# A graph network on one core: the order of three steps per window on two engines of the last stage

## The chip, the cores and the metric

One core of a Trainium2 chip runs the whole program as one launch. The metric is the device time of one execution in microseconds (us); the kernel before the change takes 5778.91 us (median of 3 runs, 5777.4 to 5779.42). The engines are TensorE (PE for matmuls, PEld for weight loads), VectorE (DVE), ScalarE (ACT), GpSimd (POOL) and SyncE (SP). DMAs are issued from the queues of ACT, POOL and SP.

## The reference

Four graph layers follow each other, each as `x = x + layer(relu(layernorm(x)))`, over 6250 nodes of 128 features and 100000 edges that are sorted by their target node `dst`. Only the last layer matters here:

```python
x_src = x[src]
msg = zeros((E, 128))
for r in range(4):                       # four kinds of edge
    hr = x_src @ weight[r] + bias[r]
    msg = where((rel == r)[:, None], hr, msg)
agg = segment_max(msg, dst, num_segments=n)     # the largest message of each target node
agg = where((deg > 0)[:, None], agg, 0)
out = x + x @ weight[4] + bias[4] + agg
```

The targets are drawn as `6250 * u ** 2`, so that low node numbers have many edges each and high ones few.

## The kernel before

A projection first writes all four products of every node into the table `y_tab` in DRAM. The last stage, which starts near 4780 us of the span, then makes the segment maximum. The edges are cut into GN = 112 groups of GE = 896 (7 tiles of 128), the nodes into NT = 49 blocks of 128. A *window* (called step `s` or `i` in the code) is one pair of a group and a block that share an edge; there are SN = 112 + 49 - 1 = 160 windows. A group whose edges all go to one block has one window, a group in which a block ends has two. As the edges thin out towards high nodes, two windows per group become more frequent towards the end.

What is done for a window `s`, and where:

- POOL gathers the 7 x 128 rows of a group from `y_tab` into a ring in `arena` that holds RG = 8 groups, with 7 indirect DMAs (L2709), and tells when the group has landed (L2703). It may overwrite a ring place once SP has seen the last window of that group staged (L2729 to L2731).
- ACT `stage_group(s)` (L2872): waits until the group has landed, then copies it from the ring to one of two buffers `staged_t`. Two windows of one group are staged twice.
- ACT `load_mask(s)` (L2879): a DMA of the row of segment borders, after the scan two windows earlier.
- PE `turn(s)` (L2835): 7 transposes to PSUM (`pa` or `pb` in turns).
- DVE `scan(s)` (L2777): a running maximum along the edges, which restarts at the borders that the mask marks. `carry_on` hands the last column on, `build(s)` (L2791) makes the 0/1 matrix that picks the last edge of each node.
- PE `back(s)` (L2842): 7 transposes of the scanned rows back to PSUM (`pc`).
- ACT `keep_back(s)` (L2883): copies them to one of two buffers `kept_t`.
- PE `select(s)` (L2849): 7 accumulating products, recorded as 14 matmuls, that move the row of each node's last edge to its node (`pd`). It waits for `keep_back(s)`, for `build(s)` and for `add(s-1)`.
- DVE `add(s)` (L2798) adds them to `x`; ACT `store(s)` (L2888) writes the block to `out`.

Each engine runs its own list in the order in which `body(i, b)` calls these functions, through `walk_steps` (L686): five calls written out, a hardware loop over pairs of windows, six calls written out. An engine does not pass over an instruction that waits. So the list sets who is held up by whom. On ACT the list of `body(i)` is stage(i+2), load_mask(i+2), keep_back(i), store(i-2). On PE it is turn(i+1), back(i), select(i-1). On DVE it is scan(i), add(i-2), carry_on(i), build(i). `window_values` (L680) at the head of ACT's body reads three numbers of the window (block, ring place, group to wait for) from a table into registers.

Of the kernel before, what the change touches and what calls it, by code (L numbers as in the profile page):

```python
# [123 lines left out]
def build(nc, a, out):  # L124
    assert QL % 2 == 0 and NT % NG == 0 and GN % RG == 0
    groups = NT // NG
    with ExitStack() as ctx:
# [221 lines left out]
        def wait_apart(engine, sem, value):  # L349


            engine.wait_ge(sem, value)
            engine.sem_inc(passed, 1)  # L353
# [311 lines left out]
        def after(engine, c, n):  # L665

            if not (isinstance(n, int) and n <= 0):
                engine.wait_ge(c.sem, c.past(n))

        def inside(s):  # L670
            return not isinstance(s, int) or 0 <= s < SN

        def loaded_values(kind, at, bounds):

            why = "the walk tables are made on the chip from counts below these bounds"
            _, values = nc.values_load_multi_w_load_instructions(at, engines=(kind,), skip_runtime_bounds_check_because=why)
            return [nc.s_assert_within(value, low, high, skip_runtime_bounds_check_because=why)
                    for value, (low, high) in zip(values, bounds)]

        def window_values(kind, table, w, first, bounds):  # L680

            last = first + len(bounds)
            at = table[0:1, w, first:last] if isinstance(w, int) else table[0:1, bass.ds(w, 1), first:last].rearrange("o w k -> o (w k)")
            return loaded_values(kind, at, bounds)

        def walk_steps(engine, body):  # L686

            for i in range(-1, 4):
                body(i, i % 2)
            with engine.Fori(2, SN // 2 - 1) as pair:  # L690
                for b in range(2):
                    body(pair * 2 + b, b)
            for i in range(SN - 2, SN + 4):
                body(i, i % 2)
# [1580 lines left out]
        with nc.Block() as block:  # L2275
# [31 lines left out]
            def _(dve):  # L2307
# [142 lines left out]
                def body(w):  # L2450
# [14 lines left out]
                    if next_here:  # L2465
                        tile, _, back = window_values(mybir.EngineType.DVE, walk_rows, w + 1, 4 * WT, AHEAD2)
                        run(w + 1, steps)
                        chain(w + 1, steps, tile, back)
# [228 lines left out]
        with nc.Block() as block:  # L2697
# [121 lines left out]
            @block.tensor  # L2819
            def _(pe):  # L2820
                def tables():
                    pe.wait_ge(table_in.sem, table_in.past(1))
                    nc.tensor.matmul(pa[:, 0:SN], ones[0:1, :], on_row, start=True, stop=True).then_inc(table_on.sem, 1)

                def relative():
                    tail = SN - P
                    pe.wait_ge(table_in.sem, table_in.past(2))
                    for j in range(GT):
                        to = (pa, pb)[j // 4][:, j % 4 * 2 * P:(j % 4 + 1) * 2 * P]
                        nc.tensor.transpose(to[:, 0:P], rel_rows[0][:, j * P:(j + 1) * P], ident[:, :])  # L2830
                        ins = nc.tensor.transpose(to[:, P:SN], rel_rows[1][0:tail, j * P:(j + 1) * P], ident[0:tail, 0:tail])
                    ins.then_inc(table_on.sem, 1)
                    pe.wait_ge(table_in.sem, table_in.past(3))

                def turn(s, b):  # L2835
                    after(pe, edge_staged, s + 1)
                    after(pe, edge_scanned, s - 1)
                    for t in range(GT):
                        ins = nc.tensor.transpose(turned_ps[b][:, t * P:(t + 1) * P], staged_t[b][:, t * P:(t + 1) * P], ident[:, :])  # L2839
                    ins.then_inc(edge_turned.sem, 1)  # L2840

                def back(s, b):  # L2842
                    after(pe, edge_scanned, s + 1)
                    after(pe, edge_kept, s)
                    for t in range(GT):
                        ins = nc.tensor.transpose(back_ps[:, t * P:(t + 1) * P], run_t[b][:, t * P:(t + 1) * P], ident[:, :])  # L2846
                    ins.then_inc(edge_back.sem, 1)

                def select(s, b):  # L2849
                    after(pe, edge_kept, s + 1)  # L2850
                    after(pe, hot_built, s + 1)
                    after(pe, block_added, s)
                    for t in range(GT):
                        ins = nc.tensor.matmul(last_ps, hot[b][:, t * P:(t + 1) * P], kept_t[b][:, t * P:(t + 1) * P],  # L2854
                                               start=(t == 0), stop=(t == GT - 1))
                    ins.then_inc(block_summed.sem, 1)

                def body(i, b):
                    if inside(i + 1):
                        turn(i + 1, 1 - b)  # L2860
                    if inside(i):
                        back(i, b)
                    if inside(i - 1):
                        select(i - 1, 1 - b)

                tables()
                relative()
                walk_steps(pe, body)

            @block.scalar  # L2870
            def _(act):
                def stage_group(s, b, start, need):  # L2872
                    after(act, edge_turned, s - 1)
                    wait_apart(act, group_landed.sem, group_landed.past(need))
                    nc.scalar.copy(staged_t[b].rearrange("p (t d) -> p t d", d=D),  # L2875
                                   ring[:, bass.ds(start, GT * RW)].rearrange("p (t w) -> p t w", w=RW)[:, :, 0:D]
                                   ).then_inc(edge_staged.sem, 1)

                def load_mask(s, b, need):  # L2879
                    after(act, edge_scanned, s - 1)  # L2880
                    act.dma_start(mask_t[b], cut_row[0:1, bass.ds((need - 1) * GE, GE)].broadcast_to([P, GE])).then_inc(mask_loaded[b].sem, 16)

                def keep_back(s, b):  # L2883
                    after(act, edge_back, s + 1)
                    after(act, block_summed, s - 1)
                    nc.scalar.copy(kept_t[b], back_ps).then_inc(edge_kept.sem, 1)  # L2886

                def store(s, j):  # L2888
                    after(act, block_added, s)
                    after(act, block_stored, s * 16)  # L2890
                    act.dma_start(out[bass.ds(j * P, P), :], x[:, bass.ds(j, 1), :].rearrange("p j d -> p (j d)")  # L2891
                                  ).then_inc(block_stored.sem, 16)

                STEP = [(0, NT - 2), (0, (RG - 1) * GT * RW), (1, GN)]

                def body(i, b):
                    if not isinstance(i, int) or 0 <= i < SN + 2:
                        j, start, need = window_values(mybir.EngineType.Activation, scalar_walk, i, 0, STEP)
                    if inside(i) and inside(i + 2):
                        stage_group(i + 2, b, start, need)  # L2900
                        load_mask(i + 2, b, need)
                    if inside(i):
                        keep_back(i, b)
                    if inside(i - 2):
                        store(i - 2, j)

                act.wait_ge(walk_laid.sem, walk_laid.past(1))
                for s in range(2):
                    start, need = loaded_values(mybir.EngineType.Activation, pe_walk[0:1, s, :], STEP[1:3])
                    load_mask(s, s, need)  # L2910
                    stage_group(s, s, start, need)
                walk_steps(act, body)
                act.wait_ge(block_stored.sem, block_stored.past(SN * 16))

# [20 lines left out]
```

## Time and profile before

| | us |
|---|---|
| median of 3 runs | 5778.91 |
| the profiled execution | 5778.91 |
| its span, first to last instruction | 5776.9 |
| last stage, first gather to the end of the span (4783.2 to 5776.9) | 993.7 |

Over the whole span PE is busy 61%, DVE 56%, ACT 34% and POOL 67%. The mean granted clock of TensorE is 0.78 of full speed, where 1.0 is the level of 2.4 GHz and 0.5 that of 1.2 GHz. In rows of a timeline, the first number is the start in us from the span's start, the second the duration; `xN` counts the instructions merged into a row, and the bracket gives the idle time of the engine before it with what ended the wait. A busy engine is not one that sets the time; the waits and the chain that ended last tell that.

### The profile page before, as it was taken

To read this page: it belongs to the slowest core of one execution; us is meant where nothing else is said; L and a number is where in the kernel's file an instruction comes from. 1 tells how busy PE (TensorE), PEld (TensorE's weight loads), DVE (VectorE), ACT (ScalarE), POOL (GpSimd) and SP (SyncE) were. 2 spreads that over 40 slices of the span, in tenths; PEclk is the share of its full clock that TensorE was granted. 3 is DMA by queue.
4 is the path that set the end of the run, shared out by engine and by line. 5 is a ranking of instruction groups with operands and counts; after the bars stand their busy time and mean duration, and the time that the engine had idled before them with its cause. 6 is when DMAs were issued, how large, how long until landed. Compare 5 with 4: busy or idle time off the path is not lost. (4 is left out here: it accounts for less than half of the span.)

```text
span 5776.9 us, 98732 instructions
## 1 busy us (share of the span) xinstructions
PE 3537.5 (61%) x18635; PEld 3062.3 (53%) x18636; DVE 3228.5 (56%) x8215; ACT 1946.2 (34%) x6380; POOL 3869.1 (67%) x4036
## 2 busy tenths in 40 slices
PE   3445556544455643889999887234555574666677
PEld 3444455544455532677777745233454544656676
DVE  4233344444455655788888863334555564455677
ACT  2111111111122211566777654123334441222333
POOL 4777777677777757777777102777777707777776
PEclk9666777766667766999999997567767787788889
DMA  4222222211111112344443220222222223333333
GB/s 124 61 61 63 64 65 65 74 52 53 52 53 52 53 38 74 107 113 116 120 118 114 88 83 23 52 53 54 53 53 52 51 79 97 93 96 101 104 112 104
DMA packets 347571, 439.10 MB, mean 76 GB/s; under 512 B 129314, under 2 KB 243822, under 8 KB 347359
## 3 DMA queue, kind: packets, MB, share of 16 engines
q0 software_dynamic: 129056, 262.08, 17.3%
q1 hardware_dynamic: 148596, 117.11, 6.4%
q10 hardware_dynamic: 69819, 58.90, 3.5%
q14 instruction: 77, 0.63, 0.0%
q8 instruction: 23, 0.38, 0.0%
HBM read 324.58 MB, written 113.18 MB: 76 GB/s over the span
## 5 line engine op out<-in xcount | busy, mean ns | idle before, releaser
L1000 PE MATMUL pa<-arena,weighted 128*128 x4480 | 866.2, 369 | 860.6 <-POOLq L719 478.4
L1000 PEld LDWEIGHTS pa<-arena,weighted 128*128 128x128 f32 x4480 | 800.1, 274 | 915.1 <-issue 915.0
L2709 POOL DMA_INDIRECT arena<-y_tab,y_idx x784 | 741.6, 946 | 395.8 <-issue 218.3
L1405 POOL DMA_INDIRECT arena<-t_tab,src_idx x784 | 778.7, 993 | 265.6 <-issue 215.8
L725 POOL DMA_INDIRECT arena<-h_tab,src_idx x784 | 743.8, 949 | 306.2 <-issue 219.5
L2288 POOL DMA_INDIRECT arena<-t_tab,src_idx x784 | 755.3, 963 | 245.0 <-issue 219.7
L725 POOL DMA_INDIRECT arena<-sage_tab,src_idx x784 | 741.0, 945 | 261.9 <-issue 214.2
L2529 PE MATMUL pa<-weighted 128*128 128x130 f32 x2240 | 421.4, 364 | 21.2 <-ACT weighted L2607 11.3
L2529 PEld LDWEIGHTS pa<-weighted 128*128 128x128 f32 x2240 | 391.7, 270 | 34.5 <-issue 19.0
L870 DVE SCALAR_TENSOR_TENSOR scan_t<-scan_t,alpha,pa 128x130 f32<-128x130 f32 x320 | 110.2, 344 | 501.7 <-PE pb L1007 351.6
L2875 ACT COPY arena<-arena 128x896 f32 x160 | 150.1, 938 | 685.7 <-POOLq L2703 613.1
L430 POOL DMA_INDIRECT start_rows<-nodeval,start_idx x98 | 101.2, 1032 | 411.7 <-DVE nodeval L2203 338.6
L862 DVE TENSOR_TENSOR weighted<-pd,rel 128x896 f32<-128x896 f32 x320 | 348.0, 1088 | 51.2 <-issue 44.6
L1045 ACT COPY out_rows<-pb 128x128 f32<-128x128 f32 x320 | 84.9, 265 | 822.3 <-PE pb L1007 701.0
L1761 PE MATMUL pa<-weighted 128*128 128x264 f32 x976 | 316.3, 407 | 58.1 <-ACT weighted L1834 38.7
L1834 ACT ACTIVATE weighted<-arena,weighted 128x128 f32 x976 | 317.4, 390 | 64.6 <-POOLq L1396 49.8
L1761 PE MATMUL pa<-arena,weighted 128*128 128x264 f32 x976 | 301.6, 391 | 50.7 <-DVE arena L1567 39.1
L2607 ACT ACTIVATE weighted<-arena,weighted 128x64 f32 x1280 | 323.0, 335 | 19.7
L2854 PE MATMUL pd<-arena,weighted 128*128 128x128 f32 x2240 | 321.9, 303 | 0.6 <-DVE x L2804 0.6
L2854 PEld LDWEIGHTS pd<-arena,weighted 128*128 128x128 f32 x2240 | 313.2, 222 | 0.8 <-issue 0.7
L1834 ACT ACTIVATE arena<-arena 128x128 f32 x976 | 307.9, 389 | 14.6
L1050 ACT ACTIVATE scan_t<-scan_t 128x128 f32<-128x128 f32 x320 | 99.0, 309 | 591.3 <-DVE scan_t L887 591.3
(553 smaller groups left out, 7440.0 us busy)
## 6 DMA issues: line engine op xcount, KB each, us to landing
gat_tab<-out_rows SPq DMA_DIRECT2D x244, 260.0 KB
mask<-cut_row ACTq DMA_DIRECT2D x160, 224.0 KB
arena<-t_tab,src_idx POOLq DMA_INDIRECT x1568
arena<-h_tab,src_idx POOLq DMA_INDIRECT x784
arena<-sage_tab,src_idx POOLq DMA_INDIRECT x784
y_tab<-arena SPq DMA_DIRECT2D x49, 256.0 KB, 2.3
arena<-y_tab,y_idx POOLq DMA_INDIRECT x784
arena<-gat_tab SPq DMA_DIRECT2D x12, 1040.0 KB, 5.0
```

The source lines that it names most:

```text
L725: nc.gpsimd.indirect_dma_start(out=rows[:, g % RG * GT + t, 0:D], out_offset=None, in_=table[:, :], in_offset=bass.IndirectOffsetOnAxis(ap ...
L862: v.tensor_tensor(hot[b].rearrange("p (t n) -> p t n", n=P), node_row.unsqueeze(1).broadcast_to([P, GT, P]), at.unsqueeze(2).broadcast_to( ...
L1000: ins = nc.tensor.matmul(pa[:, b * CE:b * CE + RW], hot[b][:, t * P:(t + 1) * P], ring[:, bass.ds(start + t * RW, RW)], start=(t == 0), st ...
L1405: nc.gpsimd.indirect_dma_start(out=rows[:, g % QR * QT + t, :], out_offset=None, in_=t1_tab[:, :], in_offset=bass.IndirectOffsetOnAxis(ap= ...
L1761: nc.tensor.matmul(pa[:, b * CE:b * CE + HALF], one, flow1[b][:, t * YW:t * YW + HALF], start=(t == 0), stop=(t == QT - 1))
L1834: ins = nc.scalar.activation(flow1[b][:, at:at + D], ring1[:, bass.ds(start + t * TW, D)], ACT.Copy, scale=flow1[b][:, t * YW + 2 * D + hd ...
L2288: nc.gpsimd.indirect_dma_start(out=rows[:, g % RB * GT + t, :], out_offset=None, in_=t2_tab[:, :], in_offset=bass.IndirectOffsetOnAxis(ap= ...
L2529: ins = nc.tensor.matmul(pa[:, b * CE:b * CE + BW], hot2[b][:, t * P:(t + 1) * P], flow[b][:, t * BW:(t + 1) * BW], start=(t == 0), stop=( ...
L2607: ins = nc.scalar.activation(flow[b][:, at:at + HD], ring2[:, bass.ds(start + t * BW + hd * HD, HD)], ACT.Copy, scale=flow[b][:, at + HD:a ...
L2709: nc.gpsimd.indirect_dma_start(out=edge_rows[:, g % RG * GT + t, 0:D], out_offset=None, in_=y_tab[:, :], in_offset=bass.IndirectOffsetOnAx ...
L2854: ins = nc.tensor.matmul(last_ps, hot[b][:, t * P:(t + 1) * P], kept_t[b][:, t * P:(t + 1) * P], start=(t == 0), stop=(t == GT - 1))
L2875: nc.scalar.copy(staged_t[b].rearrange("p (t d) -> p t d", d=D), ring[:, bass.ds(start, GT * RW)].rearrange("p (t w) -> p t w", w=RW)[:, : ...
```

## The change

Two lists are reordered, and nothing is added or removed. On PE, `select(i-1)` comes before `back(i)`. On ACT, `stage_group(i+2)` goes from the head of `body(i)` to its end, behind `load_mask(i+2)`, `keep_back(i)` and `store(i-2)`.

```diff
@@ PE
                 def body(i, b):
                     if inside(i + 1):
                         turn(i + 1, 1 - b)
+                    if inside(i - 1):
+                        select(i - 1, 1 - b)
                     if inside(i):
                         back(i, b)
-                    if inside(i - 1):
-                        select(i - 1, 1 - b)
@@ ACT
                     if inside(i) and inside(i + 2):
-                        stage_group(i + 2, b, start, need)
                         load_mask(i + 2, b, need)
                     if inside(i):
                         keep_back(i, b)
                     if inside(i - 2):
                         store(i - 2, j)
+                    if inside(i) and inside(i + 2):
+                        stage_group(i + 2, b, start, need)
```

PE in the loop over pairs of windows, before. L2839 is `turn`, L2846 `back`, L2854 `select`; L668 are the registers of their waits.

```order
L2839 MATMUL pb<-ident,arena 128x128 x7
L668 REGISTER_ALU
L2846 MATMUL pc<-ident,weighted 128x128 x7
L668 REGISTER_ALU x2
L2854 MATMUL pd<-arena,weighted 128x128 x7
L668 REGISTER_ALU
L2839 MATMUL pa<-ident,arena 128x128 x7
L2846 MATMUL pc<-ident,weighted 128x128 x7
L668 REGISTER_ALU
L2854 MATMUL pd<-arena,weighted 128x128 x7
```

The same place after the change:

```order
L2839 MATMUL pb<-ident,arena 128x128 x7
L668 REGISTER_ALU x2
L2854 MATMUL pd<-arena,weighted 128x128 x7
L668 REGISTER_ALU
L2846 MATMUL pc<-ident,weighted 128x128 x7
L668 REGISTER_ALU
L2839 MATMUL pa<-ident,arena 128x128 x7
L668 REGISTER_ALU
L2854 MATMUL pd<-arena,weighted 128x128 x7
L2846 MATMUL pc<-ident,weighted 128x128 x7
```

`back` is now the last of the three for each window, directly ahead of the next `turn`.

ACT in the last written-out call ahead of the loop, before. L676 reads the window's numbers, L2875 is `stage_group`, L2881 `load_mask`, L2886 `keep_back`, L2891 `store`.

```order
L676 TENSOR_LOAD alpha
L352 REGISTER_ALU
L2875 ISA
L2875 COPY arena<-arena 128x896
L2881 ISA
L2881 DMA mask<-cut_row 128x896
L2886 COPY arena<-pc 128x896
L2891 ISA
L2891 DMA out<-x 128x128
```

The same call after the change:

```order
L676 TENSOR_LOAD alpha
L2881 ISA
L2881 DMA mask<-cut_row 128x896
L2886 COPY arena<-pc 128x896
L2891 ISA
L2891 DMA out<-x 128x128
L352 REGISTER_ALU
L2875 ISA
L2875 COPY arena<-arena 128x896
```

The staging copy, with its waits (L352 and the ISA row), now stands behind the copy that waits for `back`.

## Rows read from the trace of the kernel before

**Rows 1.** The page: the span, and the gathers of the last stage.
```profile
span 5776.9 us, 98732 instructions
...
L2709 POOL DMA_INDIRECT arena<-y_tab,y_idx x784 | 741.6, 946 | 395.8 <-issue 218.3
```

**Rows 2.** The chain that ended last, in order of time: start, us, what.
```profile
5757.04 4.61 DMA arena<-y_tab,y_idx
```

**Rows 3.** Waits from 4820 us on: engine and line, releaser, us, times, longest.
```profile
ACT arena L2875 <- POOLq L2703: 590.7, 106, 7.1
DVE weighted L2782 <- DMA mask<-cut_row: 276.3, 90, 5.4
```

**Rows 4.** Stretches of 87.5 us, the staging copies alone (x): busy us, granted clock.
```profile
5061.80:5149.30 87.50, 12.19 (x13) 0.83 0.34 96
5149.30:5236.80 87.50, 13.14 (x14) 0.76 0.36 100
...
5324.30:5411.80 87.50, 14.08 (x15) 0.83 0.37 103
5411.80:5499.30 87.50, 15.02 (x16) 0.85 0.37 107
5499.30:5586.80 87.50, 15.96 (x17) 0.88 0.37 110
...
5674.30:5761.80 87.50, 16.89 (x18) 0.95 0.43 114
```

**Rows 5.** The same view, all: PE, PEld, DVE, ACT, POOL busy (instructions), clock.
```profile
4886.80:4974.30 87.50, 55.10 (x310) 52.90 (x309) 40.78 (x55) 19.29 (x22) 66.16 (x70) 0.75 0.31 90
4974.30:5061.80 87.50, 54.90 (x342) 52.13 (x341) 44.16 (x60) 21.04 (x24) 66.18 (x70) 0.79 0.33 93
5674.30:5761.80 87.50, 66.21 (x529) 61.69 (x527) 68.89 (x95) 31.62 (x36) 63.32 (x67) 0.95 0.43 114
```

**Rows 6.** Timeline near the end, at full clock: start, us, engine, line, operation.
```profile
5750.92 0.94 ACT L2875 COPY arena<-arena 128x896 f32 x1 [4.17 <-POOLq L2703]
...
5751.91 0.98 PE L2839 MATMUL pb<-ident,arena 128*128 128x128 f32 x7 [1.53 <-ACT arena L2875]
...
5752.81 0.95 PE L2846 MATMUL pc<-ident,weighted 128*128 128x128 f32 x7
...
5753.60 1.73 PE L2854 MATMUL pd<-arena,weighted 128*128 128x128 f32 x14
...
5755.16 0.93 PE L2839 MATMUL pa<-ident,arena 128*128 128x128 f32 x7
```

**Rows 7.** Timeline: a `back` that `keep_back` waits for, and the store behind it.
```profile
5727.29 1.70 PE L2846 MATMUL pc<-ident,weighted 128*128 128x128 f32 x7
...
5729.11 0.91 ACT L2886 COPY arena<-pc 128x896 f32<-128x896 f32 x1 [0.63 <-PE pc L2846]
5729.44 0.37 ACTq L2891 DMA_DIRECT2D out<-x  x1
```

**Rows 8.** Timeline of ACT near the stage's start: a staging copy right behind a `keep_back`.
```profile
4824.37 0.91 ACT L2886 COPY arena<-pc 128x896 f32<-128x896 f32 x1 [2.04 <-PE pc L2846]
4825.35 0.94 ACT L2875 COPY arena<-arena 128x896 f32 x1
```

**Rows 9.** Timeline of PE: `turn` after idle times of three lengths.
```profile
4841.85 0.98 PE L2839 MATMUL pa<-ident,arena 128*128 128x128 f32 x7 [1.87 <-ACT arena L2875]
...
4911.77 1.75 PE L2839 MATMUL pa<-ident,arena 128*128 128x128 f32 x7 [2.90 <-ACT arena L2875]
...
5016.83 1.10 PE L2839 MATMUL pa<-ident,arena 128*128 128x128 f32 x7 [2.56 <-ACT arena L2875]
```

**Rows 10.** Timeline of the end: the last staging, `keep_back` behind it, the last `select`.
```profile
5761.89 0.94 ACT L2875 COPY arena<-arena 128x896 f32 x1 [6.42 <-POOLq L2703]
...
5762.73 0.90 ACT L2886 COPY arena<-pc 128x896 f32<-128x896 f32 x1
...
5771.84 1.80 PE L2854 MATMUL pd<-arena,weighted 128*128 128x128 f32 x14 [0.58 <-DVE x L2804]
```

## The prediction

> **What bounds the kernel now.** Read the page first: the span, and the group of gathers of the last stage [rows 1]. 784 gathers, 946 ns each and mostly 0.3 us of issue between them, are 1.25 us apiece, so a group of 7 lands every 8.75 us. Then the chain that ended last: from about 4783 us on it is made of these gathers, down to the last one, which lands at 5757.04 + 4.61 = 5761.65 [rows 2]. So POOL sets the pace of the whole stage, and what follows the last landing is a tail of 15 us [rows 10]. The waits say the same from the other side: ACT's staging copy waits 590.7 us in 106 waits for the mark that a group has landed [rows 3]. The scans wait another 276.3 us for the mask DMA, but this lies inside the same slack.
>
> How much slack the consumers have is read from the stretches [rows 4]: in 87.5 us ten groups land, and 14 windows are staged in a stretch at 5149 to 5237, 18 in the last (13, 14, 14, 15, 16, 17, 17, 18 in the eight from 5061.8 on; one of each pair of equal counts stands in the rows). So a window may cost 87.5 / 14 = 6.25 us early and only 87.5 / 18 = 4.86 us at the end. Before 5061.8 the counts are lower still, since fewer groups have two windows. DVE needs 68.89 / 18 = 3.8 us per window [rows 5] and PE, at full clock, 0.90 + 0.79 + 1.56 = 3.25 us from `turn` to `turn` [rows 6]. Both fit.
>
> **What the change does to the loop.** Before, ACT stages window i+2 ahead of `keep_back(i)`; the staging is held up only by the landing. A `turn` is therefore ready whenever data is, and PE's three pieces of a window can run into those of the next. After, the staging of i+2 waits behind `keep_back(i)`, which waits for `back(i)`, and PE does `back(i)` last, behind `turn(i+1)` and `select(i-1)`. The next thing on PE is `turn(i+2)`, which needs that staging. This closes a ring through two engines in which nothing overlaps: turn, select, back, keep_back, staging, turn. Its period, term by term at full clock:
>
> - turn to select: 0.90 us, as from `turn` to the piece behind it, 5751.91 to 5752.81 [rows 6].
> - select to back: 1.56 us, as from `select` to the piece behind it, 5753.60 to 5755.16 [rows 6].
> - back to keep_back: the 7 transposes take 0.95 us [rows 6], and `keep_back` starts 0.12 us after their end (5727.29 + 1.70 = 5728.99, then 5729.11) [rows 7]. Together 1.07 us.
> - keep_back to staging. The trace has no staging queued behind a store. From below: 0.84 us, the distance of two copies when the second is ready (5761.89 to 5762.73) [rows 10]. From above: 0.98 us (4824.37 to 4825.35), where the table read stood between [rows 8]. The store is issued 0.33 us after `keep_back` starts and takes 0.37 us on ACT's queue [rows 7], and the waits of the staging come behind it, so I take 0.93.
> - staging to turn: 0.99 us, 5750.92 to 5751.91 [rows 6].
>
> The sum is 5.45 us per window, 5.36 to 5.50 by the bounds. The DVE's 3.8 us fit in it. The store and its wait for `add(i-2)` cost nothing: that add is needed by `select(i-1)`, which precedes `back(i)`. The mask DMA now goes out one staging earlier and is not waited for: the 276.3 us of waits should fall to nearly nothing, and win nothing, being cover under POOL. The table read of the next window is under the 3.5 us in which ACT waits for PE. On SP only the wait for `edge_staged` is touched; the ring of 8 groups gives 70 us before POOL is held up, and then POOL is late because the consumers are, not the reverse.
>
> 5.45 us is above 4.86 and below 6.25. So the windows fall behind the landings towards the end, and the backlog at the last landing is the largest value of (windows staged since some moment) x period - (time since). With 5.45 over the last 3 stretches, 52 windows: 283.4 - 262.5 = 21 us; a start inside a stretch adds up to one more window, some 25 us.
>
> **The clock in this loop.** In each period PE has one idle piece, 0.12 + 0.93 + 0.99 = 2.04 us, after 3.41 us of work. After 1.87 us of idle, `turn` still took 0.98 us, the high level (2.4 GHz); after 2.56 us it took 1.10, partly low, after 2.90 us 1.75, the low level (1.2 GHz) [rows 9]. So 2.04 lies between, nearer to the end without a fall. What speaks for a fall: the 1.87 stood alone behind work, whereas here the idle comes back each period and PE is busy 3.41 / 5.45 = 63%. The stretches in which PE is busy 55.10 / 87.5 = 63% got 0.75 and 0.79 of the clock [rows 5], though with longer idles. I take 0.79 as the granted share, 42% of the time at the low level. If that time lay all over PE's work, each us of it would lose half: period 5.45 / 0.79 = 6.90 us. Spread evenly over work and idle it is 2.04 + 3.41 / 0.79 = 6.36 us. A fall comes of an idle piece and so hits the work behind it; I take 6.8. With this the backlog is, over 7 stretches, 111 windows: 754.8 - 612.5 = 142.3 us; over 8 stretches, with 13 windows more: 843.2 - 700 = 143.2 us. Further back a stretch has under 87.5 / 6.8 = 12.9 windows and adds nothing. That is above 70 us, so POOL waits too, for the first time in this stage.
>
> The Trainium skill, TensorE: Matmul & The Clock Gate, weighs both ways. Its section "HAM oscillation — how this bites in real kernels" warns of idle gaps longer than this loop's; by that rule the clock stays high and the full-clock case below would come. The section "A second HAM failure mode: psum-queue depth-cycling" tells of a kernel whose short but frequent idles made the clock swing; by that the forecast would come. The trace of before has no run of equal short idles and decides neither.
>
> **The tail.** From the last staging to the last `select`, before: 5771.84 - 5761.89 = 9.95 us [rows 10], partly at the low clock. After, by the terms above: 0.99 + 0.90 + 1.56 + 1.07 + 1.0 + 1.56 + 1.07 + 1.0 = 9.15 us at full clock (1.0 for a `keep_back` of 0.90 and the wake-up of `select`), a little more at a lower one. The difference, -0.8 to +1, is taken as nothing.
>
> **The sum.** Span 5776.9 + 143 = 5919.9; 2.0 us lie around the span of the profiled run, whose time is also the median: 5922 us.
>
> **Rivals.**
>
> 1. The ring closes, but the clock holds. Then 5.45 us and a backlog of 25 us, with the tail 5778.9 + 25 - 0.8 = 5803 us. For it: the 1.87 us row, 0.17 us short of my idle piece. Between this and the forecast lie mixtures in which only some periods fall: at 5.85 us a period the 4 last stretches with 68 windows give 397.8 - 350 = 48 us, 5827 us.
> 2. POOL still hides everything. The time stays at 5778 +- 2, if the period in the last stretch is under 4.86 us. That needs 0.6 us less than my sum, for instance a staging copy that can start while `back` runs. Against it: an engine does not pass over the waiting `keep_back`. This is also the case in which the change does not do what I read.
> 3. Not slower but faster: with every landing met, the tail is all that could be won. The last scan no longer waits for its mask (276.3 / 90 = 3.1 us is a mean wait [rows 3]), and the `select` of the window before no longer stands ahead of the last `back` (1.56 us at full clock). Both in full: 5778.9 - 4.7 = 5774 us. It needs a period under 4.86 us, too.
> 4. Worse than forecast: granted clock 0.77 all over the work, 5.45 / 0.77 = 7.08 us, 124 windows give 877.9 - 700 = 178 us: 5957 us.
>
> **How the numbers follow.** Forecast with rival 4, 5870 to 5965: 0.62. Rival 1 at full clock 0.20, mixtures to 5870 0.12. Rival 2: 0.04, rival 3: 0.02. A difference under 0.2% (12 us) could hardly be told from none. So slower 0.94, same 0.04, faster 0.02. The range 5800 to 5965 holds all of rival 1 and the forecast; the likeliest case's own range is 5870 to 5965.
>
> **What would show it.** The wait of the staging copy for the landing should shrink from 590.7 us to less than half, none of it in the last 100 us; the idle time of PE ahead of `turn` near 2.0 us in each period of the late part; in the last stretch 5.4 us from staging to staging at full clock, 8 where the clock is low; the granted clock of the late stretches 0.77 to 0.82 instead of 0.88 to 0.95; waits for the mask near nothing; GpSimd waiting for a free ring place if the backlog passes 70 us. The forecast is wrong if late stagings still start on a landing, or if the granted clock stays above 0.9.

## The result

The changed kernel takes 5934.99 us (median of 4 runs, 5929.08 to 5937.46) against 5779.16 us (4 runs, 5777.4 to 5781.24): ratio 1.0268, interval 1.025 to 1.0286. 5922 us was predicted. The profiled execution has a span of 5927.5 us, 150.6 us more than before.

The waits from 4820 us to the end, which answer to [rows 3]:

```profile
ACT arena L2886 <- PE pc L2846: 797.8, 156, 28.4
...
PE pa L2839 <- ACT arena L2875: 173.6, 79, 5.3
...
PE pb L2839 <- ACT arena L2875: 168.4, 79, 4.0
...
POOL arena L2709 <- SPq L2731: 79.8, 19, 5.6
ACT arena L2875 <- POOLq L2703: 16.5, 10, 3.3
```

The staging copy hardly waits for a landing any more: 16.5 us where it was 590.7. ACT now waits for `back` (797.8 us, where it was 30.5), PE for the staging copy, and POOL, which never waited for a free place in the ring, waits 79.8 us for one. The waits for the mask DMA (276.3 us) are gone.

All stagings from the last one that started on a landing (5020.36) to the last of all, in the view of one stretch (busy us, count, granted clock); then all engines in the stretch of the last row of [rows 5]:

```profile
5020.00:5912.00 892.00, 122.20 (x131) 0.77 0.31 86
```

```profile
5674.30:5761.80 87.50, 62.60 (x364) 59.52 (x364) 47.31 (x65) 22.28 (x25) 50.00 (x53) 0.77 0.31 82
```

131 windows from 5020.36 to 5911.65 are 130 periods of 6.86 us in the mean. In the stretch shown POOL issues 53 gathers where it was 67, and the clock is 0.77 where it was 0.95 before [rows 4].

The end of the stage in the timeline of PE and ACT (start, duration; the bracket is the idle time before), where [rows 6], [rows 7] and [rows 10] have their counterparts:

```profile
5898.37 0.91 ACT L2886 COPY arena<-pc 128x896 f32<-128x896 f32 x1 [5.08 <-PE pc L2846]
5898.64 0.37 ACTq L2891 DMA_DIRECT2D out<-x  x1
5899.28 0.94 ACT L2875 COPY arena<-arena 128x896 f32 x1
...
5900.27 0.98 PE L2839 MATMUL pb<-ident,arena 128*128 128x128 f32 x7 [2.02 <-ACT arena L2875]
...
5901.09 1.73 PE L2854 MATMUL pd<-arena,weighted 128*128 128x128 f32 x14
...
5902.66 0.93 PE L2846 MATMUL pc<-ident,weighted 128*128 128x128 f32 x7
...
5903.70 0.91 ACT L2886 COPY arena<-pc 128x896 f32<-128x896 f32 x1 [3.48 <-PE pc L2846]
...
5904.68 0.94 ACT L2875 COPY arena<-arena 128x896 f32 x1
...
5905.67 0.98 PE L2839 MATMUL pa<-ident,arena 128*128 128x128 f32 x7 [2.08 <-ACT arena L2875]
...
5906.49 2.75 PE L2854 MATMUL pd<-arena,weighted 128*128 128x128 f32 x14
...
5909.03 1.59 PE L2846 MATMUL pc<-ident,weighted 128*128 128x128 f32 x7
...
5911.65 0.94 ACT L2875 COPY arena<-arena 128x896 f32 x1
```

Read it as a ring. At full clock it goes round in 5905.67 - 5900.27 = 5.40 us: `select` 0.82 after `turn`, `back` 1.57 later, `keep_back` 1.04 later, the staging 0.98 later, `turn` 0.99 later. Each piece follows the one ahead without a gap; on PE the next even starts some 0.15 us before the recorded end. ACT's two copies follow each other in 0.91 or 0.98 us in turns, so rounds at full clock take 5.33 and 5.40 us in turns, 5.36 in the mean.

In the next round the clock falls in the middle of `select` (2.75 us instead of 1.73), and the next `turn` starts at 5912.64, after 6.97 us. The view by stretch shows where (us, then PE, PEld, DVE, ACT, POOL busy, then the granted clock):

```profile
5900.27:5905.67 5.40, 3.31 (x29) 3.08 (x29) 3.67 (x5) 1.84 (x2) 0.00 (x0) 1.00 0.17 55
5905.67:5906.97 1.30, 1.30 (x12) 1.30 (x13) 0.28 (x1) 0.00 (x0) 0.00 (x0) 1.00 0.03 11
5907.00:5910.25 3.25, 3.25 (x17) 3.25 (x17) 2.60 (x5) 0.00 (x0) 0.00 (x0) 0.50 0.18 68
5910.50:5913.50 3.00, 0.98 (x10) 0.86 (x9) 0.55 (x1) 1.84 (x2) 0.00 (x0) 1.00 0.08 22
```

Around this round the clock is high in the idle ahead and behind, and it is low only while PE works without a break. Of the 130 periods 14 are rounds at full clock (5.33 to 5.40 us), 112 take 6.91 to 7.05 us, and 4 take longer. The fall comes at another place from round to round: `turn` takes anything from 0.98 to 1.76 us behind an idle of 2.02 or 2.08 us, and once in about nine rounds the next round stays at full clock, as here from 5709.17 to 5714.56:

```profile
5702.26 1.76 PE L2839 MATMUL pa<-ident,arena 128*128 128x128 f32 x7 [2.08 <-ACT arena L2875]
5709.17 0.98 PE L2839 MATMUL pb<-ident,arena 128*128 128x128 f32 x7 [2.02 <-ACT arena L2875]
5714.56 0.98 PE L2839 MATMUL pa<-ident,arena 128*128 128x128 f32 x7 [2.08 <-ACT arena L2875]
```

### The profile page after: what moved, and what is told of

It reads as the page before. It is cut to its first block and busy times, and to the rows that moved or that the text cites. A ratio compares the mean times of both kernels' runs of the same rounds, so it can differ in the third digit from the quotient of the medians.

```text
span 5927.5 us, 98732 instructions
## 1 busy us (share of the span) xinstructions
PE 3654.2 (62%) x18635; PEld 3174.2 (54%) x18636; DVE 3238.8 (55%) x8215; ACT 1958.6 (33%) x6380; POOL 3864.0 (65%) x4036
## 5 line engine op out<-in xcount | busy, mean ns | idle before, releaser
L2854 PE MATMUL pd<-arena,weighted 128*128 128x128 f32 x2240 | 445.5, 381 | 2.0 <-ACT arena L2886 2.0
L2854 PEld LDWEIGHTS pd<-arena,weighted 128*128 128x128 f32 x2240 | 432.1, 295 | 2.5 <-ACT arena L2886 2.5
L2886 ACT COPY arena<-pc 128x896 f32<-128x896 f32 x160 | 145.0, 906 | 813.3 <-PE pc L2846 797.8
L1763 PE MATMUL pc<-weighted 128*128 128x256 f32 x976 | 297.1, 387 | 0.0
```

Source lines behind the costliest of these rows:

```text
L1763: ins = nc.tensor.matmul(pc[:, b * CE:b * CE + 2 * D], one, flow1[b][:, t * YW + HALF:(t + 1) * YW], start=(t == 0), stop=(t == QT - 1))
```

## The experiments

All ratios are to the kernel before on the same chip (medians of 5773.65 us for the first four, 5773.34 for the last four). The times expected below count from the 5779 us of the first measurement, some 5 us more, so differences to the kernel before are compared. Two questions are open after the profile: does the loss need both edits, and how much of it is the clock?

**The PE edit alone.** ACT stages first, as before.

```diff
 PE:  turn(i + 1)
+     select(i - 1)
      back(i)
-     select(i - 1)
```

> Only PE's list is changed (select ahead of back); ACT stages first, as in the kernel before. Ring theory: the staging waits for the landing alone, so no ring closes; DVE's 3.8 us per window is the longest loop, under the 4.86 us that the last stretch allows. 5779 us, within 3 us; stagings wait about 590 us for landings, clock in the last stretch above 0.9. Rival, each order costs by itself (back now stands behind select, which waits for the add behind the scan): 1.56 us more ahead of each scan's hand-on, a period of 5.2 us or more in the last stretches and 5795 us or more.

Measured: 5774.16 us, ratio 0.9998 (0.9989 to 1.0008). The last stretch, and the wait of the staging for landings:

```profile
5674.30:5761.80 87.50, 67.13 (x507) 61.42 (x505) 66.50 (x95) 31.83 (x36) 57.57 (x61) 0.92 0.47 107
```

```profile
ACT arena L2875 <- POOLq L2703: 453.5, 85, 7.1
```

36 copies on ACT are 18 windows, as before, and the clock is 0.92. The wait for landings is 453.5 us and not the 590 expected: `back` behind `select` does eat some slack, but no time. The rival, 5795 us or more, fell.

**The ACT edit alone.** PE does turn, back, select, as before.

```diff
 ACT: load_mask(i + 2)   (stage_group(i + 2) stood ahead of it)
      keep_back(i)
      store(i - 2)
+     stage_group(i + 2)
```

> Only ACT's list is changed (staging last); PE does turn, back, select as before. Ring theory: the ring is turn 0.90, back to keep 1.07, keep to staging 0.96, staging to turn 0.99 = 3.9 us, because select lies beside ACT's two copies; under 4.86 us, so no lasting backlog: 5779 us, within 4 us. Fully at the low clock it would be 5.4 us, so some windows may lag for a moment. PE's idle in a lagging period is 0.6 us, too short for a fall. Rival, the staging's place alone is the cost: about 5930 us, as after.

Measured: 5774.27 us, ratio 0.9999 (0.999 to 1.0009). Two rounds in the late part:

```profile
5750.63 0.98 PE L2839 MATMUL pb<-ident,arena 128*128 128x128 f32 x7 [1.63 <-ACT arena L2875]
...
5751.45 0.93 PE L2846 MATMUL pc<-ident,weighted 128*128 128x128 f32 x7
...
5752.22 1.73 PE L2854 MATMUL pd<-arena,weighted 128*128 128x128 f32 x14
...
5752.49 0.91 ACT L2886 COPY arena<-pc 128x896 f32<-128x896 f32 x1 [1.92 <-PE pc L2846]
...
5753.47 0.94 ACT L2875 COPY arena<-arena 128x896 f32 x1
...
5754.46 0.98 PE L2839 MATMUL pa<-ident,arena 128*128 128x128 f32 x7 [0.52 <-ACT arena L2875]
```

The ring closes here too, but goes round in 5754.46 - 5750.63 = 3.83 us (3.9 expected), as `select` lies beside ACT's two copies. That is under the 4.86 us that the last stretch allows. So neither edit costs anything measurable; the loss is of the two together. Only then does `select` lie on the ring.

**The staging ahead of the store.** It shortens the ring and the idle of PE a little.

```diff
 ACT: load_mask(i + 2)
      keep_back(i)
+     stage_group(i + 2)
      store(i - 2)
-     stage_group(i + 2)
```

> As the changed kernel, but ACT stages ahead of the store, right behind keep_back: PE's idle per period goes from the measured 2.02 to 2.08 us to about 1.93 (keep_back to staging 0.84 instead of 0.93 to 0.97). Ring with falling clock: if the clock falls by the length of the idle, this is at the edge; periods still falling give 5.3/0.79 = 6.7 us and about 5910 us; if none falls, 5.3 us and a backlog of some 20 us, 5799 us; a mixture lies between. Theory without the clock (the ring's latencies alone): 0.1 us less per window over 131 windows, 5921 us.

Measured: 5914.24 us, ratio 1.024 (1.0223 to 1.0257). Idle and clock:

```profile
5708.05 1.09 PE L2839 MATMUL pb<-ident,arena 128*128 128x128 f32 x7 [1.91 <-ACT arena L2875]
...
5708.93 3.20 PE L2854 MATMUL pd<-arena,weighted 128*128 128x128 f32 x14
```

```profile
5674.30:5761.80 87.50, 63.73 (x362) 60.66 (x359) 47.90 (x65) 21.63 (x25) 46.46 (x50) 0.75 0.32 80
```

With 1.91 us of idle in each period the clock still falls, 0.75 in this stretch. The time is 141 us over the kernel before, where the first theory had 131 and the one without the clock 142, so it does not tell them apart; the next run does.

But the clock does not fall in every round. Five rounds in a row, from 5319.62 to 5345.75, take 5.22 or 5.23 us at full clock, with the same 1.91 us ahead of each `turn`; the six behind them take 6.86 or 6.87 us:

```profile
5324.85 0.98 PE L2839 MATMUL pb<-ident,arena 128*128 128x128 f32 x7 [1.91 <-ACT arena L2875]
...
5330.07 0.98 PE L2839 MATMUL pa<-ident,arena 128*128 128x128 f32 x7 [1.91 <-ACT arena L2875]
```

```profile
5319.62:5345.75 26.13, 16.56 (x141) 15.38 (x141) 18.36 (x25) 8.72 (x10) 19.73 (x22) 1.00 0.41 109
5345.75:5387.00 41.25, 29.77 (x169) 28.35 (x169) 22.39 (x30) 10.46 (x12) 31.19 (x34) 0.75 0.38 95
```

So the length of the idle does not decide it for a single round. What does is not shown.

**Seven idle-filling transposes.** They come behind `back` and write where the next `turn` will write over them.

```diff
                     if inside(i):
                         back(i, b)
+                        for _ in range(7):
+                            nc.tensor.transpose(turned_ps[b][:, 0:P], ident[:, :], ident[:, :])
```

> As the changed kernel, with 7 transposes of the identity added on PE behind each back, into the PSUM half that the next turn overwrites (work that nothing reads). PE's idle per period goes from 2.04 to 1.27 us at full clock; the ring itself is untouched, since the filler ends before the staging does. Clock theory: the clock stays high, the period is 5.4 us, the backlog 25 us: 5803 us (5797 to 5812), granted clock in the last stretches above 0.95. Rival, the loss is the ring's latency and not the clock: 5930 us or more.

Measured: 5793.63 us, ratio 1.0034 (1.0021 to 1.0047). Two rounds and the last stretch:

```profile
5722.26 0.93 PE L2866 MATMUL pb<-ident 128*128 128x128 f32 x7
...
5724.45 0.98 PE L2839 MATMUL pb<-ident,arena 128*128 128x128 f32 x7 [1.26 <-ACT arena L2877]
...
5725.27 1.73 PE L2854 MATMUL pd<-arena,weighted 128*128 128x128 f32 x14
...
5726.83 0.93 PE L2846 MATMUL pc<-ident,weighted 128*128 128x128 f32 x7
...
5729.84 0.98 PE L2839 MATMUL pa<-ident,arena 128*128 128x128 f32 x7 [1.32 <-ACT arena L2877]
...
5735.17 0.98 PE L2839 MATMUL pb<-ident,arena 128*128 128x128 f32 x7 [1.26 <-ACT arena L2877]
```

```profile
5674.30:5761.80 87.50, 65.78 (x566) 61.75 (x564) 60.04 (x82) 31.13 (x34) 58.36 (x62) 1.00 0.41 102
```

The ring still takes 5729.84 - 5724.45 = 5.39 and then 5.33 us, the clock is 1.00 from 5412 to 5762 us, and what is left of the loss is 0.34%, some 20 us (24 expected; the 5803 us themselves missed, as the kernel before took 5 us less). Against the changed kernel's 1.0268 the filler takes back 2.34% of 5774 us, 135 us. So the ring costs 20 us at full clock, and the clock that falls in it 135. A low clock costs this only on the closed ring: it is low in the kernel before too (0.76 to 0.88 in the stretches up to 5587 [rows 4]), and POOL hides it there.

**Three, and one.** The same loop with `range(3)` and `range(1)`.

> As the changed kernel, with 3 transposes of the identity behind each back. PE's idle per period goes from 2.02 to 2.08 us to about 1.7, below the 1.87 us after which the kernel before still had the high clock. Clock theory, by the length of the idle: the clock holds as with 7 of them, 5794 us (5791 to 5798). Rival, what counts is the share of PE work in a period (66% here, 61% without, 73% with 7): the clock still swings in part, 5820 to 5900 us.

> As the changed kernel, with one transpose of the identity behind each back: idle about 1.9 to 2.0 us, the same as in the run that stages ahead of the store (1.91), whose clock fell. Clock theory: it falls here too, the period of 5.4 us at full clock stays, and the time is that of the changed kernel or a little less, 5900 to 5935 us. If the edge lies in between, a mixture of some 5830 us.

Measured: with three 5796.38 us, ratio 1.0035 (1.0022 to 1.0049); with one 5910.57 us, ratio 1.0233 (1.0217 to 1.0248). `turn` and the stretch 5674 to 5762 with three:

```profile
5723.56 0.98 PE L2839 MATMUL pb<-ident,arena 128*128 128x128 f32 x7 [1.69 <-ACT arena L2877]
...
5728.95 0.98 PE L2839 MATMUL pa<-ident,arena 128*128 128x128 f32 x7 [1.75 <-ACT arena L2877]
```

```profile
5674.30:5761.80 87.50, 58.89 (x502) 55.10 (x503) 59.19 (x81) 30.44 (x33) 66.17 (x70) 1.00 0.42 107
```

and with one:

```profile
5722.19 1.62 PE L2839 MATMUL pa<-ident,arena 128*128 128x128 f32 x7 [1.98 <-ACT arena L2877]
...
5729.16 0.98 PE L2839 MATMUL pb<-ident,arena 128*128 128x128 f32 x7 [1.91 <-ACT arena L2877]
```

```profile
5674.30:5761.80 87.50, 62.22 (x384) 59.08 (x383) 49.17 (x66) 23.97 (x26) 50.09 (x53) 0.79 0.32 85
```

With 1.69 to 1.75 us of idle per round the clock is 1.00 in this stretch; with 1.91 to 1.98 us it is 0.79. (The profiled execution with three took 5804.21 us, the slowest of its five; its gathers of this stage start 9 us later than with seven.) No version with the closed ring lies between the two in this stretch, but with one transpose 22 of 113 rounds from 5144 us on run at full clock (5.33 to 5.40 us), between rounds of 6.96 to 7.04, with the same idles. The rival that counts PE's work expected a mixture with three, and none came. But work and idle change together here, so the runs do not separate the two as causes.

**Both: staging ahead of the store, and seven transposes.**

```diff
 PE:  back(i), then 7 transposes
 ACT: load_mask(i + 2), keep_back(i), stage_group(i + 2), store(i - 2)
```

> As the changed kernel, with the staging ahead of the store and 7 transposes of the identity behind each back: full clock and a ring shorter by 0.12 us (5.27 instead of 5.39). Backlog theory: over the last 56 windows (the stretch in which it builds up) 0.12 x 56 = 6.7 us less than with the 7 transposes alone, 5787 us (5784 to 5790). Rival, what is left of the loss there is a longer tail and not a backlog: 5793 us.

Measured: 5788.61 us, ratio 1.0024 (1.0015 to 1.0033).

```profile
5721.92 0.98 PE L2839 MATMUL pb<-ident,arena 128*128 128x128 f32 x7 [1.15 <-ACT arena L2877]
...
5727.14 0.98 PE L2839 MATMUL pa<-ident,arena 128*128 128x128 f32 x7 [1.15 <-ACT arena L2877]
```

The ring is 5.22 us. The time lies where the backlog puts it: 5787 us was expected, 6.7 us less than with seven transposes alone, and the distance to the kernel before shrank from 20.0 to 15.3 us. But the intervals of this run and of the one with seven transposes alone overlap, so it agrees with the backlog and does not prove it.

**The mask ahead of the landing, in the kernel before.**

```diff
 ACT:
+    load_mask(i + 2)
     stage_group(i + 2)
-    load_mask(i + 2)
     keep_back(i)
     store(i - 2)
```

> The kernel before with one edit on ACT: load_mask ahead of stage_group, so that the mask DMA no longer waits for the landing. The scans' 276 us of waits for the mask go away. Theory (POOL hides all but the tail): 5773 us, at most 2 us less. Rival, the mask waits were worth something: 5760 us or less.

Measured: 5775.24 us, ratio 1.0002 (0.9993 to 1.0011). Its waits for landings stay as they were; below them the waits of the scans:

```profile
ACT arena L2875 <- POOLq L2703: 588.7, 100, 27.5
...
DVE weighted L2782 <- PE pa L2839: 112.5, 38, 5.4
...
DVE weighted L2782 <- PE pb L2839: 97.2, 39, 4.9
```

The waits for the mask, 276.3 us in sum [rows 3], are gone and were worth nothing: the scans now wait for `turn` instead. No version tried is faster than the kernel before.

## Why the prediction was right

- *The ring.* Right, and shown: with either edit undone the time is that of before, with both it is 1.0268. Its period at full clock was put at 5.45 us and is 5.33 or 5.40 in turns, 5.36 in the mean. `turn` to `select` is 0.82 us and not 0.90. The 0.90 was misread: it held a wait, since `back` there also needs the `keep_back` of the window before, which ended at 5751.76 + 0.90 = 5752.66, just ahead of `back` at 5752.81. (The row of it in the trace of before: `5751.76 0.90 ACT L2886 COPY arena<-pc 128x896 f32<-128x896 f32 x1`.) With the ACT edit alone, where `back` follows `turn` too, it is 0.82. The other terms are within 0.05 us, and keep_back to staging, which no row showed, is 0.91 or 0.98 us in turns (0.93 was taken).
- *The clock.* Right, and this was the weakest step: the trace of before had 1.87 us without a fall and 2.56 with part of one, and 2.04 us was nearer to the first. It fell, to 0.77 over 892 us (0.79 was taken). That the two are so close is in part luck, as 0.79 was read from stretches with longer idles. The period then is 6.86 us (6.8 taken). 5.36 / 0.77 = 6.96 would be all low time over work; spread evenly over work and idle it would be 2.05 + 3.31 / 0.77 = 6.35. So nearly all of it lies over the work, as taken. The argument for it holds only in part: the clock does not fall right behind the idle, but at a place that shifts from round to round, 1.3 us into the work in the round shown. Nor is a round ever low throughout: the 8 us that were expected from staging to staging at the low clock are 6.91 to 7.05. And that the idle comes back in each period, which was the reason given for a fall, is not enough: with three or seven transposes it comes back too, 1.75 or 1.32 us long, and the clock is 1.00.
- *The backlog.* Put at 143 us. The last staging starts 5911.65 - 5761.89 = 149.8 us later than before. The 7 us are the period, 0.06 us over some 124 windows. The backlog began at 5020.36 and not at 5061.8, which is worth nothing, since there the landings and the ring are about equally fast.
- *POOL held up for the first time.* Right, 79.8 us in 19 waits, as the backlog passes the 70 us that the ring of 8 groups holds. It is a consequence: the consumers have data all the time.
- *The tail.* Taken as nothing. From the last staging to the end of the span it is 5776.9 - 5761.89 = 15.0 us before and 5927.5 - 5911.65 = 15.9 us after.
- *The rival "the clock holds"* was priced at 5803 us, 24 us over before. The runs with the clock held by transposes show 20 and 23 us. So had the clock held, some 5800 us would have been the result.
- *POOL hides everything* needed a period under 4.86 us, and each edit alone is that case (3.83 us on the ring for the ACT edit). The mask's waits, put at nothing, are shown to be worth nothing.

The Trainium skill, TensorE: Matmul & The Clock Gate, warns in its section "HAM oscillation — how this bites in real kernels" only of idle gaps longer than these. Here the measurement differs: idles of 1.91 to 2.08 us in each round brought the clock down in three kernels. Its section "A second HAM failure mode: psum-queue depth-cycling" tells of short idles between groups of matmuls that come often enough to make the clock swing between its two levels. The trace agrees, with 1.00 and 0.50 by turns in the round shown above.

## What to carry to other kernels

When engines work through lists of their own, a reordering is priced by the rings that it closes: follow each wait from engine to engine until it comes back, add the terms, and compare with the time that the slowest feeder leaves at its tightest place, not on average. Two reorderings that are free alone can put a piece on the ring together. And once TensorE idles in every round, ask what its clock will do: here the ring cost 0.3% and the clock in it 2.3%, and 3 useless transposes per window bought the 2.3% back. A mean period can hide two kinds of rounds, so look at single rounds before giving a reason for the mean.

## What the runs showed of the hardware

TensorE got faster at its real work by being given more: 0.33 us of transposes that nothing reads, per 5.4 us round, moved the granted clock of the stretch from 5674 to 5762 us from 0.77 to 1.00 and the time from 1.0268 to 1.0035 of before. In the means over that stretch lies a step: with idle of 1.75 us per round the clock is 1.00, with 1.91 us or more it is 0.75 to 0.79. Yet the length of the idle alone does not make a round slow: with staging ahead of the store, five rounds in a row kept full clock with 1.91 us each, and in the kernel before `turn` ran at the high level after a single 1.87 us [rows 9]. What else decides, the runs leave open.

The clock fell and rose inside PE's unbroken work, 1.3 us and some 4.7 us behind the start of `turn` in the round from 5905.67, while it was 1.00 in the idle ahead. So a slow `select` or `back` is not a sign of an idle piece directly in front of it.
